# A fused attention and expert kernel: a new order of work in a slot, and one more gate on GpSimd

## What is computed

```python
x = x + attention(ln_c(x))        # windows of 8x8 tokens, 4 heads of 16 channels, relative bias
t = tokens(x)                     # (4, 16384, 64)
t = t + moe(ln_t(t))              # 8 experts of 64x64, router softmax, the best 2, shares made to sum to 1
x = image(t)

def attention(xw):                # xw: (windows, 64 tokens, 64 channels)
    q, k, v = heads(xw @ Wq + bq), *heads2(xw @ Wkv + bkv)
    a = softmax(q * 16**-0.5 @ k.T + bias)
    return (a @ v) @ Wproj + bproj

def moe(x):
    top_p, top_i = top_k(softmax(x @ router_w + router_b), 2)
    return sum_k(top_p / sum(top_p) * (x @ expert_w[top_i] + expert_b[top_i]))
```

## Time and profile before

| what | value |
|---|---|
| median of 3 runs | 1300.76 us (1299.04 to 1303.33) |
| the profiled execution | 1299.6 us, span 1297.8 us |
| granted TensorE clock, mean over the span | 0.982 of full speed |
| PE busy | 1173.9 us, 90% of the span |
| DVE busy | 1094.1 us, 84% |
| GpSimd busy | 1006.7 us, 78% |
| ACT busy | 885.5 us, 68% |

### The profile page before, as it was taken

How to read it: one execution, slowest core, us unless ns; L and a number is a source line. 1 busy time by engine, 2 the same in 40 slices (tenths; PEclk the granted TensorE clock), 3 DMA queues, 4 the chain that set the end, 5 groups by cost and what they waited for, 6 DMA issues and landing times.

```text
span 1297.8 us, 47440 instructions
## 1 busy us (share of the span) xinstructions
PE 1173.9 (90%) x19715; PEld 735.2 (57%) x19840; DVE 1094.1 (84%) x2311; ACT 885.5 (68%) x1679; POOL 1006.7 (78%) x861
## 2 busy tenths in 40 slices
PE   3679999999999999999999999999999999999985
PEld 2555656655565665655566556555656565656541
DVE  6558898898888889899888888989988888888874
ACT  5467777767766777767676777776767666766642
POOL 6367888889777888888877788888877787778652
PEclk8589999999999999999999999999999999999999
DMA  7012333322222333322222333332222222222221
GB/s 202 2 37 75 82 90 84 81 61 66 54 61 76 82 81 92 86 60 65 64 54 64 90 78 84 92 77 53 69 61 57 58 68 61 60 61 61 60 69 41
DMA packets 95621, 91.42 MB, mean 70 GB/s; under 512 B 26928, under 2 KB 62384, under 8 KB 95408
## 3 DMA queue, kind: packets, MB, share of 16 engines
q1 hardware_dynamic: 95408, 88.37, 26.9%
HBM read 35.90 MB, written 17.83 MB: 41 GB/s over the span
## 4 chain that ended last, share of the span: by engine, by line
PE 58%; DVE 13%; ACT 11%; issue 9%; POOL 1%; DMA 1%; SPq 0%; another core or an unknown queue 0%; ACTq 0%; DVEq 0%; POOLq 0%
PE bank_y L528 14%; PE bank_s L409 9%; PE bank_t L424 8%; PE bank_s L383 7%; DVE t_g L983 5%; PE bank_o L437 4%; PE bank_p L452 4%; ACT k_m L653 4%; PE bank_g L516 4%; DVE x L899 3%; DVE mx L878 2%; PE bank_p L516 2%; ACT prob_t L677 2%; PE bank_e L472 1%; PE bank_t L361 1%
## 5 line engine op out<-in xcount | busy, mean ns | idle before, releaser
L1113 POOL TENSOR_TENSOR prob<-prob,mx 128x512 f32<-128x512 f32 x256 | 261.5, 1042 | 47.5 <-DVE mx L878 47.5
L528 PE MATMUL bank_y<-t_g,w_exp 128*64 128x512 f32 x1024 | 275.9, 616 | 24.6 <-DVE t_g L983 23.3
L1135 POOL TENSOR_TENSOR t_g<-t_t,g_copy 128x512 f32<-128x512 f32 x128 | 165.5, 1293 | 142.9 <-ACT g_copy L710 141.8
L673 ACT ACTIVATE prob<-prob 128x512 f32<-128x512 f32 x256 | 162.0, 633 | 145.1 <-POOL prob L1113 145.1
L871 DVE TENSOR_TENSOR prob<-bank_s,rel 128x1024 f32<-128x1024 f32 x128 | 156.5, 1222 | 39.9 <-PE bank_s L409 34.9
L983 DVE TENSOR_TENSOR t_g<-t_t,bank_p 128x512 f32<-128x512 f32 x256 | 174.1, 680 | 15.2 <-PE bank_p L516 10.1
L424 PE MATMUL bank_t<-idn,prob 128*128 128x128 f32 x1024 | 165.8, 285 | 21.6 <-ACT prob_t L677 11.5
L424 PEld LDWEIGHTS bank_t<-idn,prob 128*128 128x128 f32 x1024 | 113.7, 142 | 89.9 <-ACT prob L673 49.3
L677 ACT ACTIVATE prob_t<-bank_t 128x512 f32<-128x512 f32 x256 | 153.3, 599 | 6.3 <-PE bank_t L424 6.1
L878 DVE TENSOR_REDUCE mx<-prob 128x16 f32<-128x1024 f32 x128 | 154.9, 1210 | 0.1
L409 PEld LDWEIGHTS bank_s<-k_m,q_t 32*64 32x64 f32 x4096 | 113.9, 135 | 71.3 <-issue 62.4
(11 more groups left out here) (122 smaller groups left out, 2313.9 us busy)
## 6 DMA issues: line engine op xcount, KB each, us to landing
t_t<-t_rout SPq DMA_DIRECT2D x256, 128.0 KB, 2.3
x_in<-in_x SPq DMA_DIRECT2D x68, 256.0 KB, 3.3
r_b<-recip_rows SPq DMA_DIRECT2D x64, 256.0 KB
out_y<-y_out SPq DMA_DIRECT2D x128, 128.0 KB, 2.4
r_in<-sum_b SPq DMA_DIRECT2D x64, 16.0 KB
recip_rows<-r_out SPq DMA_DIRECT2D x64, 16.0 KB, 1.4
gate_sel<-in_sel SPq DMA_DIRECT2D x1, 512.0 KB, 3.5
rel<-in_relb SPq DMA_DIRECT2D x1, 256.0 KB, 3.1
```

What stands on the lines that cost most here:

```text
L528: mm(B_Y[C * a:C * a + C, :], w_exp[:, pair, :], t_g[:, (2 * pair + a) % TG, :], start=False, stop=(pair == MIXES // 2 - 1), skip_group_ch ...
L673: A(prob[:, i], prob[:, i], ACT.Exp).then_inc(p_ready.sem, 1)
L1113: G.tensor_tensor(sc, sc, mx[:, i, :].unsqueeze(2).broadcast_to([P, 2 * HEADS, NTOK]), ALU.subtract).then_inc(s_shifted.sem, 1)
L1135: G.tensor_tensor(t_g[:, u % TG, :], t_t[:, p, u % 2, :], g_copy[:, n % 2, :], ALU.mult).then_inc(tg_pool.sem, 1)
```

## The change

Four things change at once. On PE, `prob_sums` of group j-1 now comes directly behind `scores(j, 1)`, then the first turn of probabilities, then keys and values, and only then `values`; `turn_values` comes ahead of gate 7. A second buffer of prob_t (index p) makes that order possible. On DVE, `normalise` now stands ahead of `bias(j+1, 0)`, and gate 5 behind `maxima(j+1, 0)`. Expert 4's gate is made by GpSimd, for which ACT copies its bank. ACT copies the values and the second keys early; the result of a slot is copied out and stored early in the next slot, and on SP the store now stands between `cut_sums` and `spread_reciprocals`. The two new buffers take the place of gate_sel, which now shares memory with t_g.

```diff
-ON_POOL = (2, 6)
+ON_POOL = (2, 4, 6)
...
-        prob_t = sb("prob_t", [P, UNITS, HEADS, P])
+        prob_t = sb("prob_t", [P, 2, UNITS, HEADS, P])
...
# SP, slot
                 if outputting:
                     cut_sums(j - 1)
+                if j > 3:
+                    store(j - 4)
                 if outputting:
                     spread_reciprocals(j - 1)
...
-                if mixing:
-                    store(j - 3)
...
# PE, slot
                 if outputting:
-                    values(j - 1, 1 - p)
-                    prob_sums(j - 1)
+                    prob_sums(j - 1, 1 - p)
+                if attending:
+                    turn_probs(j, 0, work)
                 if projecting:
                     project(j + 1, KEYS_VALUES)
-                if attending:
-                    turn_probs(j, 0, work)
+                if outputting:
+                    values(j - 1, 1 - p)
...
                     project_out(j - 1)
-                if mixing:
-                    gates(j - 3, 7)
                 if projecting:
                     turn_values(j + 1, attending)
                 if mixing:
+                    gates(j - 3, 7)
...
# ACT, slot
                     copy_sums(j - 1)
+                if attending:
+                    copy_probs(j, p, 0)
+                if j > 3:
+                    copy_result(j - 4)
                 if projecting:
                     copy_k(j + 1, 1 - p, 0)
-                if attending:
-                    copy_probs(j, 0)
+                    copy_k(j + 1, 1 - p, 1)
+                    if not work.take:
+                        copy_v(j + 1)
...
+                if mixing:
+                    copy_gates(j - 3, 4)
...
# DVE, slot
                     gate(j - 3, 1 - p, 3)
-                    gate(j - 3, 1 - p, 4)
+                if outputting:
+                    normalise(j - 1)
                 if projecting:
                     bias(j + 1, 0)
-                if outputting:
-                    normalise(j - 1)
+                    maxima(j + 1, 0)
                 if mixing:
                     gate(j - 3, 1 - p, 5)
-                if projecting:
-                    maxima(j + 1, 0)
...
# GpSimd, slot
                     normalise_input(j + 2)
                 if mixing:
+                    gate(j - 3, 1 - p, 4)
                     gate(j - 3, 1 - p, 6)
```

More of the change, by code:

```diff
@@ L151, in build @@
         t_g = sb("t_g", [P, TG, BANK])
-        g_copy = sb("g_copy", [P, 2, BANK])
+        gate_sel = t_g[:, 0:2, :].rearrange("p n (m q) -> p (n m) q", q=P)
+        g_copy = sb("g_copy", [P, len(ON_POOL), BANK])
         y_out = sb("y_out", [P, 4, W])
@@ L342, in _ @@
             pipeline(sp, slot, lambda batch, t, r: None, lambda batch: None, lambda batch: None)
+            store(LAST)
             sp.wait_ge(stored, BATCH * STRIPS * 32 + 1)
@@ L437, in values, with prob_sums @@
                             last = mm(B_O[rows, at:at + NTOK], v_bd[:, p, i, b, h, :],
-                                      prob_t[:, i, h, b * NTOK:(b + 1) * NTOK], start=True, stop=True,
+                                      prob_t[:, p, i, h, b * NTOK:(b + 1) * NTOK], start=True, stop=True,
                                       skip_group_check=True)
                 last.then_inc(o_done.sem, 1)
-            def prob_sums(g):
+            def prob_sums(g, p):
+                pe.wait_ge(pt_ready.sem, pt_ready.at(g, 4))
                 if not (isinstance(g, int) and g == 0):
@@ L451, in prob_sums @@
                         dst = B_P[rows, :].rearrange("p (b i q) -> p b i q", b=2, i=UNITS)[:, :, i, :]
-                        last = mm(dst, ones_bd[:, :], prob_t[:, i, h, :].rearrange("p (b q) -> p b q", b=2),
+                        last = mm(dst, ones_bd[:, :], prob_t[:, p, i, h, :].rearrange("p (b q) -> p b q", b=2),
                                   start=True, stop=True, skip_group_check=True)
@@ L673, in exps, with copy_probs @@
                 A(prob[:, i], prob[:, i], ACT.Exp).then_inc(p_ready.sem, 1)
-            def copy_probs(g, i):
+            def copy_probs(g, p, i):
                 act.wait_ge(pt_done.sem, pt_done.at(g, i + 1))
-                A(prob_t[:, i].rearrange("p h q -> p (h q)"), B_T[:, :], ACT.Copy).then_inc(pt_ready.sem, 1)
+                A(prob_t[:, p, i].rearrange("p h q -> p (h q)"), B_T[:, :], ACT.Copy).then_inc(pt_ready.sem, 1)
             def copy_sums(g):
@@ L709, in copy_gates @@
                 act.wait_ge(gate_done[u % 2].sem, gate_done[u % 2].at(g, u // 2 + 1))
-                A(g_copy[:, ON_POOL.index(u) % 2, :], B_G[:, :], ACT.Copy).then_inc(g_copied.sem, 1)
+                A(g_copy[:, ON_POOL.index(u), :], B_G[:, :], ACT.Copy).then_inc(g_copied.sem, 1)
             def copy_result(g):
@@ L732, in slot @@
                     copy_tokens(j - 2)
+                if projecting and work.take:
+                    copy_v(j + 1)
+                if attending and not work.take:
+                    copy_probs(j, p, 1)
+                if routing_on:
                     copy_logits(j - 2)
-                if projecting:
-                    copy_v(j + 1)
-                if attending:
-                    copy_probs(j, 1)
+                if attending and work.take:
+                    copy_probs(j, p, 1)
                 if attending:
@@ L745, in slot @@
                     exps(j, 3)
-                    copy_probs(j, 2)
+                    copy_probs(j, p, 2)
+                if mixing:
+                    copy_gates(j - 3, 4)
                 if routing_on:
@@ L754, in slot @@
                 if attending:
-                    copy_probs(j, 3)
+                    copy_probs(j, p, 3)
                 if work.take:
@@ L766, in slot @@
                     exps(j + 1, 1)
-                if mixing:
-                    copy_result(j - 3)
             pipeline(act, slot, first_take, first_root, lambda batch: None)
+            copy_result(LAST)
         @block.vector
@@ L1134, in gate @@
                 pool.wait_ge(y_done.sem, y_done.at(g, max(u - TG + 1, 0)))
-                G.tensor_tensor(t_g[:, u % TG, :], t_t[:, p, u % 2, :], g_copy[:, n % 2, :],
+                G.tensor_tensor(t_g[:, u % TG, :], t_t[:, p, u % 2, :], g_copy[:, n, :],
                                 ALU.mult).then_inc(tg_pool.sem, 1)
```

3 lines of the change are left out of this document (removed).

## The result

The changed kernel takes **1270.1 us** (median of 4 runs, 1268.81 to 1271.72) against 1300.63 us before (1299.04 to 1303.33); the ratio is 0.9764 with a 95% interval of 0.9744 to 0.9784. The profiled execution took 1268.81 us with a span of 1267.0 us, 30.8 less than before, at nearly the same granted clock (0.983 on the mean, 0.982 before).

A forecast was written before the change was run, and what follows sets the result against it. PE first, with DVE and ACT holding it up; DVE's line ends plain slots. Gains of 10.6 us (34 plain) and 18.6 (24 take), less 2 for totals, make 27: 1299.6 to 1272.6, forecast 1273, range 1252 to 1302.

The forecast's parts named there:

- the one with the 0.52: Forecast case, chance 0.52: 1273 us, its own part 1263 to 1283, by a late share between 0.15 and 0.6.
- DVE's line behind the scores: Plain slot's second half: bias, normalise, gate 5, maxima, add_input and gate 7 on DVE end the slot; gain 0.69 us.
- is no longer in the way: DVE behind gate 3: without gate 4 (0.69 us), normalise starts when r_b has landed, t 11.55.
- the walk: Step through one plain slot's timelines, starting at 1083.83: new length 17.81 us, or 18.87 with late reciprocals.
- The round trip is uncovered: Reciprocals through DRAM: r_b at 12.96 makes a plain slot 0.36 us worse, a take slot still 0.55 better.
- the forecast's shares: Weights for plain and take slots: 0.64 with the fast gain, 0.36 with late reciprocals.
- land no sooner: Sums come 0.9 us earlier, but DVE reaches the reciprocals behind maxima(j, 1) as before, so r_b is not earlier.
- The first half is worth nothing: Slot's start on PE: keys and values start earlier, but turn_tokens still waits for t_n until 5.98; value 0.
- ACT's order fits: ACT's new copy order: g_t starts at 5.82, ends at 6.42, just in time; cost 0. Too-slow rival: 1288, chance 0.08.
- GpSimd bounds the take slots at 18.5: Third gate makes GpSimd's loop about 18.5 us, the new bound in take slots; gain 0.9 against 19.44.
- the late share: Share of the 58 slots with a reciprocals' write over 2 us: 21/58 = 0.36.
- No port lock: Rival, chance 0.02: GpSimd's new gate and DVE lock each other out, up to 1.29 us in 58 slots, 1375 us.

The follow-up runs named there:

- the start alone: Changed kernel with gate 4 back on DVE and DVE's order bias, normalise, gate 5, maxima; 1286.78 us, 0.9896 of the kernel before.

## Why the prediction was right, and where it was not

Forecast were 1273 us and a gain of 27; measured were 1270.1 and 30.5, and the case that came is the one with the 0.52: most of a fast slot's gain, less what late reciprocals take. The mechanism of the plain slots was right. Part of the agreement is luck: take slots were to give 18.6 us and gave 18.7, but by a bound that the runs refute, and the other slots' 11.0 against 8.6 is made of several errors with both signs.

- **DVE's line behind the scores ended the slot.** Right: putting the bias first again costs 18 us, and PE is now busy for nearly all of a fast plain slot. Forecast 17.81, measured 17.94. The 0.13 is already there when the output projection starts (forecast 13.97, measured 14.10); from there to the next scores both have 3.84. What holds the usual plain slot at 17.94 wasn't in the sum and is shown in part only: PE has 0.14 us of idle time left, but 0.22 us less work on it saved 0.06.
- **Gate 4 "is no longer in the way".** Wrong for plain slots, as two runs show: moved alone it brings nothing, and taken back it costs 0.08 there. The step only looked right because the walk let normalise start at 11.55, and no start before about 11.9 shortens the slot; with the gate on DVE it starts at 11.81. Its worth, 0.56 us, lies in the slots with a sum of squares, and there only with the normalisation first.
- **The round trip is uncovered, and a late write costs.** Right in mechanism, too large in size. The walk gave 18.87 for a normalisation at 12.96, which is 5.91 from there to the end; measured are 6.03. But the write was late by less: SP's next DMA behind r_b started at 12.67 at the latest, 11.66 on the mean in plain slots, and these came to 18.07 on the mean against 18.19 by the forecast's shares. That the reciprocals "land no sooner" was off as well: the write is issued at 5.97 on the mean in plain slots, where it was 6.26. Before, the sums' read stood behind the store on SP (at 1086.44 and 1087.61 in the slot of the earlier trace rows), and DVE waited 19.7 us for it in 25 slots; now it is 6.8 us in 6.
- **The first half is worth nothing.** Right as to the tokens' turn, which moved by only 0.09, and the queries' 0.12 against 0.18. Wrong as to the sum of it: the term stood at nothing, and the start alone is worth 14 us, 0.14 in each plain slot and 0.35 in each take slot. I walked only a plain slot and put one number on the take slots.
- **ACT's order fits.** Right: g_t starts at 5.70 in the fast slot, where 5.82 was forecast.
- **GpSimd bounds the take slots at 18.5.** Wrong. 0.75 us less work in them changed nothing. Their length came near (18.71 against 18.67 by the late share) for another reason: in the 21 with a sum of squares DVE comes to its normalisation at 12.67 and in all but one doesn't wait for r_b, and the slot ends 6.06 later. The three without it end at 18.1 to 18.6 whether gate 4 is on DVE or not, so what they share, the turned image on PE and ACT, seems to stand close behind.
- **The slots with the variances** were counted as plain. With five more operations on GpSimd in them, they came out 0.80 longer instead; 2.4 us. With gate 4 back on DVE they are at 18.66. The same slot before had GpSimd busy for 16.95 us:

```profile
596.02:614.61 18.59, 17.64 (x308) 10.91 (x312) 16.81 (x37) 15.44 (x28) 16.95 (x18) 1.00 0.26 62
```

- **No port lock**: GpSimd's gates keep their 1292 ns, with a third one among them. By the rule of the Trainium skill's page "SBUF — State Buffer" (section "Who interferes with whom") DVE's multiplies, which read one of their inputs from PSUM, don't contend with GpSimd; the trace agrees (1265 to 1315 ns over the 192 gates).

Why the writes were late by less than before can be read from the two traces, though no run moved the cause by itself. 23 of the 64 writes took over 2 us in both kernels, with a mean of 2.90 us before and 2.50 after, and over 2.8 us took 16 before and 3 after. All 23 late ones, in both, had an instruction packet on the DMA engines between 0.4 and 1.4 us behind their issue; of the 41 others only 7 did before and 4 after. Before, the queue 8 packet had started behind the issue of every late write that had one (by 0.26 us or more); after, in 13 of the 23 it had started ahead of the issue, and these took 2.41 on the mean. The size of this may change with any edit that moves the write against the packets; that the gain came out above the forecast and not below is luck in this respect. No view shows whose instructions the packets of queue 8 carry. It was not tried to move the packets, nor to spread the reciprocals without DRAM.

## What to carry to other kernels

Walk each kind of slot by itself: an engine with a hole in the common slot may be the bound in the slot with extra work, and a move may pay only there. When a consumer is moved ahead of the work that hid its input, look up how that input's arrival spreads, not only when it came in one slot; doubling the suspected DMA in both versions measures the cover in one run each. An edit that does nothing alone, or loses, may be half of one that gains: the wait behind the one removed decides. And read the usual slot beside the mean: a few late DMAs moved the mean of the plain slots by more than the edit under test did.

## What the runs showed of the hardware

From the issue of a 16 KB write to DRAM until SP went on behind it took 1.41 us at the least and 3.40 at the most in the kernel before, 1.41 and 3.29 in the changed one. Every one of the 23 that took over 2 us, in either, had an instruction packet on the DMA engines meanwhile, of queue 8 in 21 and 22 cases. One added write and its wait cost 56.6 us in 64 slots, 0.88 each. ACT's operations follow each other closer than their own duration: the two key copies of 0.77 us took 1.45 together, so a row of copies must be costed by starts.
